# Graph layer on one core: edge-MLP operands of 30 rows padded to 128, and the products with edge attributes divided anew between VectorE and ScalarE

## What is computed

```python
h = jax.nn.silu(edge_length_embedded @ W_mlp1 / math.sqrt(N_BASIS))
ew = h @ W_mlp2 / math.sqrt(N_HID)
wa, wb, wc, wd = (ew[:, :MUL], ew[:, MUL:2 * MUL], ew[:, 2 * MUL:3 * MUL], ew[:, 3 * MUL:])
m0a = wa * g0 * y0[:, None]
m0b = wb * jnp.einsum('eum,em->eu', g1, y1) / math.sqrt(3.0)
m1a = wc[:, :, None] * g0[:, :, None] * y1[:, None, :]
m1b = wd[:, :, None] * g1 * y0[:, None, None]
s_mid = jax.ops.segment_sum(jnp.concatenate([m0a, m0b], axis=1), edge_dst, num_segments=N)
v_mid = jax.ops.segment_sum(jnp.concatenate([m1a, m1b], axis=1), edge_dst, num_segments=N)
```

## Time and profile before

| | us |
|---|---|
| median of three runs | 4400.84 |
| lowest, highest | 4399.68, 4402.47 |
| span of the profiled execution | 4400.9 |
| PE busy | 4086.7 (93%) |
| PEld busy | 3374.9 (77%) |
| DVE busy | 2987.8 (68%) |
| ACT busy | 2610.6 (59%) |
| POOL busy | 2599.1 (59%) |

### The profile page before, as it was taken

How to read it: one execution, slowest core, us unless ns; L and a number is a source line. 1 busy time by engine, 2 the same in 40 slices (tenths; PEclk the granted TensorE clock), 3 DMA queues, 4 the chain that set the end, 5 groups by cost and what they waited for, 6 DMA issues and landing times. The chain is left out here.

```text
span 4400.9 us, 84837 instructions
## 1 busy us (share of the span) xinstructions
PE 4086.7 (93%) x19450; PEld 3374.9 (77%) x19450; DVE 2987.8 (68%) x5419; ACT 2610.6 (59%) x8831; POOL 2599.1 (59%) x2378
## 2 busy tenths in 40 slices
PE   4999599999999999999999999999985888888887
PEld 3888488888888888888888888888985777777776
DVE  5666699999999999999999999997666000000000
ACT  1444587888788878887888787776232222222222
POOL 3444577777777777777777777775113233333332
PEclk8999799999999999999999999999967999999999
DMA  3333333443444333433443444433223455555554
GB/s 117 103 101 98 116 103 103 104 104 103 104 104 104 104 104 104 103 103 104 104 104 103 103 103 104 104 103 85 79 80 107 147 153 152 155 161 156 152 161 119
DMA packets 432067, 497.39 MB, mean 113 GB/s; under 512 B 253111, under 2 KB 343707, under 8 KB 417707
## 3 DMA queue, kind: packets, MB, share of 16 engines
q0 software_dynamic: 105984, 260.17, 22.1%
q1 hardware_dynamic: 326059, 236.92, 18.8%
HBM read 433.72 MB, written 63.07 MB: 113 GB/s over the span
## 5 line engine op out<-in xcount | busy, mean ns | idle before, releaser
L615 POOL DMA_INDIRECT k_x<-gather_table,edges_src x1760 | 1995.9, 1134 | 576.9 <-issue 446.4
L632 ACT ACTIVATE k_x<-k_x,edges_y 128x64 f32<-128x64 f32 x5280 | 1303.0, 335 | 4.9 <-DMA k_x<-gather_table,edges_src 4.9
L738 PE MATMUL edges_ps_sum<-k_x,edges_hot_y 128*128 128x256 f32 x3520 | 1094.2, 393 | 0.5 <-issue 0.5
L738 PE MATMUL edges_ps_sum<-k_x,edges_hot 128*128 128x256 f32 x3520 | 1048.1, 379 | 0.0
L639 ACT ACTIVATE edges_hot_y<-edges_hot,edges_y 128x128 f32<-128x128 f32 x1760 | 562.4, 390 | 506.9 <-DVE edges_hot L678 506.9
L727 PE MATMUL edges_ps_edge<-k_w_e,edges_hT 100*128 100x256 f32 x3520 | 836.4, 380 | 7.8 <-ACT edges_hT L625 7.8
L694 DVE TENSOR_TENSOR k_x<-k_x,edges_ps_edge 128x768 f32<-128x768 f32 x880 | 794.4, 941 | 0.0
L738 PEld LDWEIGHTS edges_ps_sum<-k_x,edges_hot_y 128*128 128x128 f32 x3520 | 633.6, 190 | 175.3 <-issue 107.1
L727 PEld LDWEIGHTS edges_ps_edge<-k_w_e,edges_hT 100*128 100x128 f32 x3520 | 670.8, 191 | 101.5 <-issue 7.6
L738 PEld LDWEIGHTS edges_ps_sum<-k_x,edges_hot 128*128 128x128 f32 x3520 | 670.0, 190 | 91.1
L1341 DVE TENSOR_TENSOR experts_raw<-experts_ps_y,experts_b 128x256 f32<-128x256 f32 x112 | 42.3, 419 | 908.7 <-PE experts_ps_y L1297 908.7
(11 more groups left out here) (233 smaller groups left out, 3996.6 us busy)
## 6 DMA issues: line engine op xcount, KB each, us to landing
experts_w<-in_w SPq DMA_DIRECT2D x112, 1024.0 KB
k_x<-gather_table,edges_src POOLq DMA_INDIRECT x1760
edges_el<-el_hi SPq DMA_DIRECT2D x880, 20.0 KB
edges_el<-el_lo SPq DMA_DIRECT2D x440, 20.0 KB
nodes_el<-in_el SPq DMA_DIRECT2D x46, 170.0 KB, 2.4
el_hi<-nodes_el_hi SPq DMA_DIRECT2D x46, 170.0 KB, 1.9
el_lo<-nodes_el_lo SPq DMA_DIRECT2D x46, 170.0 KB, 2.0
experts_b<-in_b SPq DMA_DIRECT2D x56, 128.0 KB
```

The source lines that it names most:

```text
L615: nc.gpsimd.indirect_dma_start(out=rows[k][:, j, :], out_offset=None, in_=K.table_d.rearrange("t p d -> (t p) d"), in_offset=bass.Indirect ...
L632: x = nc.scalar.activation(Z[k % 2][:, j, MUL * (i + 1):MUL * (i + 2)], rows[k][:, j, 0:MUL], ACT.Identity, scale=y[k][:, j, 1 + i:2 + i])
L738: x = t.matmul(into[:, :, o, :], rows_hot[k % 2][:, j, :], msg[k % 2][:, j, o * D:(o + 1) * D], start=j == 0 and o == 0, stop=j == GC - 1, ...
```

## The change

- `el` and `w_e1s`, the operands of L721, grow from 30 to 128 partitions. The added rows are zero: POOL clears the four `el` buffers once at the stage's start, and SP's first load waits for that; `w_e1s` is cleared in `setup`. Each item's loads still write 30 rows.
- `Z` and `dot3` lie side by side in one tile of 448 columns, `of_factors`. The twelve ACT scalings per item now each write two blocks of 64 columns: `g0` times `y1[i]` into `Z`, and `g1[i]` times `y1[i]` into `dot3`. The DVE product L672 is gone.
- ACT scales two of the four one-hot chunks into `hot_y`; DVE does the other two in one instruction after `dot`.
- On DVE `dot2` and `dot` move behind the vectors, and the wait for the gathered rows moves from before `dot3` to before the first scalars. PE waits for the second half of `hot_y` too.

```diff
 def edges(nc, A, K, acc):
-        el, src, dst = four("el", [3 * BAS, GE], f32r), four("src", [P, GC], i32), four("dst", [P, GC], i32)
+        el, src, dst = four("el", [P, GE], f32r), four("src", [P, GC], i32), four("dst", [P, GC], i32)
...
+        of_factors = [part((8 * D + k * 7 * MUL) * GC, 7 * MUL) for k in range(2)]
+        Z = [x[:, :, 0:D] for x in of_factors]
+        dot3 = [x[:, :, D:].rearrange("p c (i u) -> p c i u", i=3) for x in of_factors]
+        dot2 = [part((8 * D + 14 * MUL + k * MUL) * GC, MUL) for k in range(2)]
...
+            sp.wait_ge(c["blank"], 4)
             steps(sp, NI, 4, 0, body)
...
+            for k in range(4):
+                nc.gpsimd.memset(el[k][:, :].bitcast(f32), 0.0).then_inc(c["blank"], 1)
             steps(pool, NI, 4, 0, body)
...
                 for j in range(GC):
                     for i in range(3):
-                        x = nc.scalar.activation(Z[k % 2][:, j, MUL * (i + 1):MUL * (i + 2)], rows[k][:, j, 0:MUL],
+                        x = nc.scalar.activation(blocks(of_factors[k % 2][:, j, :])[:, i + 1:i + 5:3, :],
+                                                 blocks(rows[k][:, j, :])[:, 0:i + 2:i + 1, :],
                                                  ACT.Identity, scale=y[k][:, j, 1 + i:2 + i])
                 x.then_inc(c["factors"], 1)
...
-                for j in range(GC):
+                for j in range(GC // 2):
                     x = nc.scalar.activation(hot_y[k % 2][:, j, :], hot[k % 2][:, j, :], ACT.Identity, scale=y[k][:, j, 0:1])
...
-                dve.wait_ge(gathered[k], per(n, k, 64, 4))
-                dve.wait_ge(c["dot"], n)
-                v.tensor_tensor(dot3[h][:, :, :, :], rows[k][:, :, MUL:D].rearrange("p c (i u) -> p c i u", i=3),
-                                y[k][:, :, 1:4].unsqueeze(3).to_broadcast([P, GC, 3, MUL]),
-                                ALU.mult).then_inc(c["dot3"], 1)
...
-                dve.wait_ge(c["dot3"], n + 1)
-                v.tensor_tensor(dot2[h][:, :, :], dot3[h][:, :, 0, :], dot3[h][:, :, 1, :],
-                                ALU.add).then_inc(c["dot2"], 1)
-
+
+                dve.wait_ge(gathered[k], per(n, k, 64, 4))
                 dve.wait_ge(c["weights"], n + 1)
...
                 scalars(0, rows[k])
-                dve.wait_ge(c["dot2"], n + 1)
-                dve.wait_ge(c["messages"], n + 3)
-                v.tensor_tensor(Z[h][:, :, 0:MUL], dot2[h][:, :, :], dot3[h][:, :, 2, :], ALU.add).then_inc(c["dot"], 1)
                 vectors(0, rows[k])
                 dve.wait_ge(c["factors"], n + 1)
+                v.tensor_tensor(dot2[h][:, :, :], dot3[h][:, :, 0, :], dot3[h][:, :, 1, :],
+                                ALU.add).then_inc(c["dot2"], 1)
                 vectors(1, Z[h])
+                dve.wait_ge(c["dot2"], n + 1)
+                v.tensor_tensor(Z[h][:, :, 0:MUL], dot2[h][:, :, :], dot3[h][:, :, 2, :], ALU.add).then_inc(c["dot"], 1)
+                dve.wait_ge(c["hot"], n + 1)
+                rest = slice(GC // 2, GC)
+                v.tensor_tensor(hot_y[h][:, rest, :], hot[h][:, rest, :],
+                                y[k][:, rest, 0:1].to_broadcast([P, GC - GC // 2, P]), ALU.mult).then_inc(c["hot_y_rest"], 1)
                 dve.wait_ge(c["dot"], n + 1)
                 scalars(1, Z[h]).then_inc(c["messages"], 1)
...
                 pe.wait_ge(c["hot_y"], n + 1 + FREE)
+                pe.wait_ge(c["hot_y_rest"], n + 1)
```

More of the change, by code:

```diff
@@ L107, in setup @@
         m = Mem(nc, ctx, "setup")
-        loaded, made, scaled = m.sem("loaded"), m.sem("made"), m.sem("scaled")
+        loaded, made, scaled, blank = m.sem("loaded"), m.sem("made"), m.sem("scaled"), m.sem("blank")
         w_hi, low_row, w_part = m.sb("w_hi", [3 * BAS, HID], f32r), m.sb("low_row", [3 * BAS, 1]), m.sb("w_part", [3 * BAS, HID])
@@ L133, in _ @@
             g.memset(K.minus_half[:, :], -0.5)
+            g.memset(K.w_e1s[:, :].bitcast(f32), 0.0).then_inc(blank, 1)
             g.memset(K.eps[:, :], EPS)
@@ L166, in _ @@
             dve.wait_ge(scaled, 3)
-            nc.vector.tensor_copy(K.w_e1s[:, :], w_part[:, :]).then_inc(scaled, 1)
+            dve.wait_ge(blank, 1)
+            nc.vector.tensor_copy(K.w_e1s[0:3 * BAS, :], w_part[:, :]).then_inc(scaled, 1)
 def items(nc, A, K):
@@ L581, in edges @@
         cut = lambda at, n: room[:, at * GC * D:(at + n) * GC * D].rearrange("p (c n) -> p c n", c=GC)
-        rows, Z, msg = [cut(k, 1) for k in range(4)], [cut(4 + k, 1) for k in range(2)], [cut(6 + 2 * k, 2) for k in range(2)]
-        dot3 = [cut(10 + k, 1)[:, :, 0:3 * MUL].rearrange("p c (i u) -> p c i u", i=3) for k in range(2)]
-        dot2 = [cut(10 + k, 1)[:, :, 3 * MUL:] for k in range(2)]
+        rows, msg = [cut(k, 1) for k in range(4)], [cut(4 + 2 * k, 2) for k in range(2)]
+        part = lambda at, w: room[:, at:at + GC * w].rearrange("p (c n) -> p c n", c=GC)
+        of_factors = [part((8 * D + k * 7 * MUL) * GC, 7 * MUL) for k in range(2)]
+        Z = [x[:, :, 0:D] for x in of_factors]
+        dot3 = [x[:, :, D:].rearrange("p c (i u) -> p c i u", i=3) for x in of_factors]
+        dot2 = [part((8 * D + 14 * MUL + k * MUL) * GC, MUL) for k in range(2)]
         ps_e = [m.ps(f"edge{k}", 2) for k in range(2)]
@@ L587, in edges @@
         loaded, gathered = ([m.sem(f"{x}{k}") for k in range(4)] for x in ("loaded", "gathered"))
-        c = {x: m.sem(x) for x in ("cleared", "messages", "flushed", "hidden", "act", "weights", "factors", "rel", "hot_y",
-                                   "dot3", "dot2", "dot", "hot", "summed", "passed")}
+        c = {x: m.sem(x) for x in ("blank", "cleared", "messages", "flushed", "hidden", "act", "weights", "factors", "rel", "hot_y",
+                                   "hot_y_rest", "dot2", "dot", "hot", "summed", "passed")}
         block = ctx.enter_context(nc.Block())
@@ L629, in body @@
                 act.wait_ge(c["messages"], n + 3)
+                blocks = lambda a: a.rearrange("p (b u) -> p b u", u=MUL)
                 for j in range(GC):
                     for i in range(3):
-                        x = nc.scalar.activation(Z[k % 2][:, j, MUL * (i + 1):MUL * (i + 2)], rows[k][:, j, 0:MUL],
+                        x = nc.scalar.activation(blocks(of_factors[k % 2][:, j, :])[:, i + 1:i + 5:3, :],
+                                                 blocks(rows[k][:, j, :])[:, 0:i + 2:i + 1, :],
                                                  ACT.Identity, scale=y[k][:, j, 1 + i:2 + i])
@@ L1377, in program @@
         K.w_e1, K.w_e2 = sb("w_e1", [3 * BAS, HID]), sb("w_e2", [HID, 256])
-        K.w_e1s = sb("w_e1s", [3 * BAS, HID], f32r)
+        K.w_e1s = sb("w_e1s", [P, HID], f32r)
         K.w_lo0, K.w_lo1 = sb("w_lo0", [P, MUL]), sb("w_lo1", [P, MUL])
```

## The result

Median of three runs: 4274.66 us (4250.76 to 4292.51), before 4400.84; ratio 0.971, 95% interval 0.966 to 0.976. That is 43 us more than the 4232 forecast, inside the range, and within 4 us of what the rival "gathers take over" gave. The profiled execution is the longest of the three, with a span of 4290.8 and a time of 4292.51. In the code after the change L728 is the old L721 (first layer), L734 the weights, L746 the sums, L641 ACT's scalings with edge attributes, L621 the gathers, L682 hot, L701 and L705 the two steps of the dot product, L708 DVE's half of `hot_y`.

What follows compares the result with a forecast made beforehand. PE was taken to bound the edge stage at 5.78 us per item, with 0.39 of gaps around L721. The sum was 4400.9 - 171 (padding) + 1.7 (start) = 4232 us, range 4224 to 4315.

Steps and rivals of the forecast that it cites:

- gathers take over: Rival: POOL's gathers, meeting DVE's two-operand instructions at random, set a period of 5.48 us; 4271 us, chance 0.14.
- What bounds before: Edge stage: PE sets the pace at 5.78 us per item, 0.39 of it gaps around L721, likely from its rows.
- Padding: PE, edge stage: 128 rows remove all gaps, 5.78 to 5.39 us per item, 171 us in all.
- 0.11, 0.19 and 0.10: PE's gaps in us: before L721, from L721 to L738, and in the first pair of L738.
- half the gap stays: Rival: the L721 to L738 time belongs to the single-pass matmul; period 5.57 us, 4311 us, chance 0.08.
- DVE: DVE per item: L672 goes (-0.87 us), the `hot_y` half adds 0.37, so 5.38 becomes 4.88 us.
- ACT: ACT per item: two-block scalings at 0.30 us each, 4.77 us in all.
- It is hidden: ACT's silu and scalings for the next item end at 6.7 us, 1.3 into the next period; DVE wants them at 3.3.
- POOL: Gathers take 5.20 us per item, 5.77 with stretch; without L672, hot's 0.2 us wait lets POOL keep up with 5.39.
- Start: Start of the edge stage: four clears hold back the first load, adding 1.7 us.
- no effect: Rival: rows do not matter, PE still paces at 5.78 us, DVE's savings stay hidden; 4403 us, chance 0.08.
- two blocks cost two: Rival: 0.48 us per ACT scaling makes ACT the bound at 6.93 us per item; 4905 us, chance 0.03.

Runs made afterwards that it cites:

- move alone: The change without the padding (30 rows, products moved): 4405.05 us, ratio 1.001 to the kernel before.
- padding alone: The kernel before with only `el` and `w_e1s` at 128 rows and their clears: 4241.41 us, ratio 0.965; again beside the change, 4243.18 us.
- all on ACT: The change with all four chunks of `hot_y` scaled by ACT and no half on DVE: 4244.35 us, ratio 0.964 to the kernel before.
- f4_tensor_scalar_hot: The change with hot and DVE's half of `hot_y` made by tensor_scalar instructions with one SBUF tensor operand: 4279.31 us, ratio 0.973 to the kernel before.

## Why the prediction came out as it did

*What bounds before: right.* PE set the pace, and rows were the cause of the gaps (64 against 96 rows).

*Padding: right, slightly too large.* The sum had 5.39; the floor is 5.41 to 5.42, 0.36 per item recovered. How it was split was wrong: of 0.11, 0.19 and 0.10 the first measured 0.28, the second nothing, the third 0.10. So the 0.40 from L721 to L738 was no gap, as the rival "half the gap stays" had said, and yet the rival's 5.57 did not come, because the 1.72 taken for L727 ahead of L721 was too long: with 96 or 128 rows L728 starts 1.55 after it. That the total came out near 5.39 is in part luck. Gains on DVE and ACT alone bought nothing, as move alone shows.

*DVE: the pitches were right, the sum and its worth were not.* The half of `hot_y` has a pitch of 0.33 against 0.37 taken, but from flush to flush DVE needs 5.27 and not 4.88: the flush doesn't follow the last scalars, it starts 1.35 after dot, where the sum had 1.15, and hot, now right behind rel, starts 0.26 after it (L672 stood there at 0.13). I costed the lighter DVE as a help since it had "0.01 us to spare at 5.39". Padding alone reaches 5.41 with DVE 1394 of 1400 busy: what little there was to spare was enough.

*ACT: the price was right, the cover wrong.* Twelve scalings of two blocks take 3.62, or 0.30 each, as taken. "It is hidden" failed: 0.86 us of waiting for gathers per item stood in front of them, and silu behind them, so that PE waited for silu.

*POOL: the step that failed.* "Where the gather that starts in hot waits only its last 0.2 us, POOL keeps up with 5.39." It looked at the one longest blocker that was left and forgot that the others can be met too. In the change all four are, 0.26 to 0.32 us per item, against 0.2 of room. The rival had 0.28 by counting random meetings, and so 4271; with 0.14 it was given far too little. Its reason was only half right: padding alone and all on ACT show that meetings need not be random, and then POOL does keep up, so that its time came within 4 us is in part luck.

*Start: right.* Four clears took 1.92 us, and from ACT's first record of the stage to PE's first L728 it is 7.1 us instead of 5.2.

```profile
486.60 1.92 POOL L626 MEMSET edges_el<- 128x512 f32 x4 [23.18 <-POOLq L282]
```

*Sum.* PE's first to last L721 took 2545.1 us before, and L728's 2432.2: 113 less where 171 was forecast. Of the missing 58, 0.03 x 438 = 13 is the floor, and the rest, 0.1 per item, is the gathers' pace. This is the longest of the three runs; by the medians 126 came off where 169 was forecast. The runs side by side price the gathers at 35 (4279.84 - 4244.35).

*The rivals* "half the gap stays", "no effect" and "two blocks cost two" did not happen. Of the signs named for wrong, the period above 5.45 was seen; PE did wait, though for silu and not for messages or factors. Of those named for right, L728 within 1.73 of L734 and the first pair of 0.43 were seen; the 0.21 from L728 to L746 was not (0.42).

## What to carry over

When a small matmul of 64 rows or fewer stands between large ones, look for gaps on both sides of it in PE's timeline, and pad its rows (96 were enough here). When such a gap is closed, work out again which engines had room only because of it: here POOL, with 0.2 us of 5.41, for which no row said how it would fall in. Then test each part of a change alone: here the padding brought all of the gain, the long product's move nothing (all on ACT 4244.35, padding alone 4243.18), and the half of `hot_y` on DVE took 35 us back.

## What the runs showed of the hardware

- One matmul of 30 or 64 rows among matmuls of 100 and 128 costs 0.36 us, 0.28 ahead of it and the rest behind it in the next group; 96 and 128 rows cost nothing.
- A gather issued by POOL under a DVE instruction with two SBUF operands ends 0.95 us after that instruction gives way; without such an instruction it takes 1.00, with 0.30 to the next. Under an instruction with one operand in PSUM it takes at most 0.01 more, under one with a single SBUF tensor and a scalar per partition (hot in `f4_tensor_scalar_hot`) at most 0.10.
- Where POOL and DVE meet at such a place, the wait per item is not fixed: for one and the same product it was 0.56 us in the kernel before, 0.20 with the padding, and 0.28 in the padding's long run (4241.41 against 4283.14 us).
- ACT's activation over 128 columns in two blocks takes 0.30 us, as one of 128 columns in one piece.
